# Summing the projection of an attention layer in half-height TensorE tiles, with denser keys

## The reference

```python
qk = jnp.einsum('bhwc,oc->bhwo', x, W_qk) + b_qk      # q: 4 heads x 64, k: 32 channels
...
attn = jnp.einsum('bxyhcp,bxyhdp->bxyhcd', q, k)      # sum over the 64 pixels p of a window
attn = attn * temperature[None, None, None, :, None, None]
```

## Time and profile before

| what | us |
|---|---|
| median of 3 runs | 1118.27 |
| lowest and highest | 1116.99, 1118.3 |
| the profiled execution's own time | 1117.37 |
| its span, first to last instruction | 1115.4 |
| TensorE matmul busy, VectorE busy | 888.9, 845.1 |

### The profile page before, as it was taken

One profiled execution on the slowest core, in us unless ns is written; L12 is line 12 of the kernel. 1 busy time (PEld: TensorE's weight loads), 2 busy tenths in 40 slices (PEclk: granted clock), 3 DMA queues, 4 the chain that ended last, 5 costly groups with the idle time before them and its releaser, 6 DMA issues. The chain is left out here.

```text
span 1115.4 us, 21429 instructions
## 1 busy us (share of the span) xinstructions
PE 888.9 (80%) x6876; PEld 591.1 (53%) x6876; DVE 845.1 (76%) x1207; ACT 600.1 (54%) x695; POOL 324.9 (29%) x265
## 2 busy tenths in 40 slices
PE   5699986979997667965999949799966588676774
PEld 4343336978875465343433349788854563233332
DVE  7577787987868844885778879877778446799796
ACT  5899982323333153546999923233332444466564
POOL 0000008500009910510000067000089304465564
PEclk8899997989998678988999969999986688899897
DMA  9100000000000020242000000000000200033334
GB/s 304 36 1 0 0 0 1 0 1 1 0 1 2 1 75 3 72 139 88 0 0 0 0 1 1 1 1 0 1 2 2 75 0 1 0 114 113 113 113 151
DMA packets 51305, 39.40 MB, mean 35 GB/s; under 512 B 1600, under 2 KB 50880, under 8 KB 51008
## 3 DMA queue, kind: packets, MB, share of 16 engines
q1 hardware_dynamic: 51264, 38.85, 11.0%
HBM read 22.07 MB, written 16.78 MB: 35 GB/s over the span
## 5 line engine op out<-in xcount | busy, mean ns | idle before, releaser
L333 PE MATMUL ps<-work,cst 128*128 128x512 f32 x512 | 235.9, 608 | 17.3 <-ACT work L547 13.5
L333 PEld LDWEIGHTS ps<-work,cst 128*128 128x128 f32 x512 | 94.3, 193 | 157.6 <-issue 143.4
L547 ACT ACTIVATE work<-X,l0s 128x2048 f32 (+1 forms) x64 | 136.7, 2141 | 3.8 <-SPq L291 3.8
L253 PE MATMUL ps<-ST,work 128*128 128x512 f32 (+1 forms) x256 | 131.7, 638 | 7.5 <-DVE work L866 5.4
L554 ACT ACTIVATE work<-ps 128x2048 f32<-128x2048 f32 x64 | 123.1, 1924 | 7.1 <-PE ps L333 6.8
L988 POOL TENSOR_TENSOR work<-cst,ksum 128x512 f32<-128x512 f32 x64 | 69.5, 1105 | 174.5 <-SPq L291 172.6
L778 DVE TENSOR_TENSOR work<-ps,cst 64x512 f32<-64x512 f32 x128 | 88.1, 688 | 37.8 <-PE ps L400 36.0
L953 POOL TENSOR_TENSOR co<-mv,cst 128x1 f32<-128x1 f32 x8 | 1.5, 189 | 383.0 <-DVEq L243 296.7
L576 ACT ACTIVATE work<-ps 128x512 f32<-128x512 f32 x80 | 47.8, 597 | 99.6 <-PE ps L353 99.6
L1023 POOL TENSOR_TENSOR work<-X,work 128x512 f32<-128x512 f32 x64 | 82.1, 1286 | 58.9 <-DVE work L913 58.9
L364 PE MATMUL ps<-cst,work 128*128 128x143 f32 x640 | 96.5, 296 | 1.4 <-DVE X L728 1.2
(11 more groups left out here) (96 smaller groups left out, 1649.3 us busy)
## 6 DMA issues: line engine op xcount, KB each, us to landing
work<-x SPq DMA_DIRECT2D x32, 512.0 KB, 4.6
out<-work SPq DMA_DIRECT2D x64, 256.0 KB, 2.8
work<-choose SPq DMA_DIRECT2D x2, 2048.0 KB, 7.9
cst<-consts SPq DMA_DIRECT2D x1, 1009.5 KB, 9.0
cst<-consts SPq DMA_DIRECT2D x1, 64.0 KB, 1.9
```

Of the source, the lines that this page charges most:

```text
L253: return nc.tensor.matmul(ps[:, bank, :], sel[:, n, :], ST[:, ds(s * (4 * H), 4 * H)], start=True, stop=True)
L333: last = pe.matmul(ps[:, 4 * (m % 2) + b, :], wg[:, m, :], yb[:, m, b * BANK:(b + 1) * BANK], start=True, stop=True)
L547: act.activation(yb[:, m, :], X[:, ds(s * PIX + i * CHUNK, CHUNK)], ACT.Gelu, scale=l0s[:, m:m + 1], bias=l0s[:, MULTI + m:MULTI + m + 1]) ...
```

## The change

M is summed by one matmul for each pair, each half of the pixel rows and each image: 64 rows by 32 columns of the array, 33 columns moved. The upper half of the pixel rows gives the first window of a pair, the lower half the second, and each half has a PSUM bank of its own (4 + 2u + hp). The keys of a pixel are then just 32 numbers and a one, so `kh` has 33 columns where it had 128, `keys` is one operation over 128 partitions, and GpSimd sets only the ones. `copy_m` reads two banks in one operation. TensorE's middle banks are written out instead of looped.

```diff
@@ -138,7 +138,7 @@
         mall, _e0 = part(0, [NWIN, NWIN, C + 1])
         xn, _e = part(_e0, [RING, NWIN, WS, WS])
         xw, _e = part(_e, [RING, 4, P])
-        kh, _e = part(_e, [RING, 4, G, P])
+        kh, _e = part(_e, [RING, 4, G, C + 1])
 
         rs, _e = part(_e0, [RING, NWIN, P])
         qb, _ = part(_e, [RING, WS, NWIN // 2, WS])
@@ -190,7 +190,7 @@
         s_x1 = rsem("z_added", "dve")
         s_strip = sem("strip_ready")
         s_next = rsem("next_strip_ready", "pool")
-        s_zero = sem("keys_buffers_zeroed")
+        s_ones = sem("keys_ones_set")
         s_pt = sem("patches_transposed")
         s_pc = rsem("patches_copied", "act", DEEP)
         s_cv = rsem("pair_filtered", "pe", 2 * DEEP)
@@ -406,16 +406,18 @@
                     pe.wait_ge(s_kh, after(nn))
                     pe.wait_ge(s_mc, slot(nn))
                     for pp in range(4):
-                        for g in range(G):
-                            last = pe.matmul(ps[C * g:C * g + C, 4 + u, pp * P:pp * P + P],
-                                             xw[:, u, pp, C * g:C * g + C], kh[:, u, pp, g, :],
-                                             start=True, stop=True)
+                        for hp in range(2):
+                            rows = slice(N * hp, N * hp + N)
+                            for g in range(G):
+                                last = pe.matmul(ps[C * g:C * g + C, 4 + 2 * u + hp, pp * (C + 1):(pp + 1) * (C + 1)],
+                                                 xw[rows, u, pp, C * g:C * g + C], kh[rows, u, pp, g, :],
+                                                 start=True, stop=True)
                     last.then_inc(s_m, 1)
 
                 project(0, 0, 0, 0)
                 project(0, 1, 0, 1)
                 m_sum(0, 0)
-                with pe.Fori(0, 7) as i:
+                for i in range(7):
                     for u in range(2):
                         w1 = i * 2 + (u + 1)
                         project(w1, w1 * 2, 1 - u, 0)
@@ -588,8 +590,8 @@
                 def copy_m(n, u):
                     nn = s * NB + n
                     act.wait_ge(s_m, after(nn))
-                    src = ps[:, 4 + u, :].rearrange("p (a b) -> p a b", b=N)[:, :, 0:C + 1]
-                    dst = work[:, ds(n * (8 * (C + 1)), 8 * (C + 1))].rearrange("p (a b) -> p a b", b=C + 1)
+                    src = ps[:, 4 + 2 * u:6 + 2 * u, 0:4 * (C + 1)].rearrange("p hp (a b) -> p a hp b", b=C + 1)
+                    dst = work[:, ds(n * (8 * (C + 1)), 8 * (C + 1))].rearrange("p (a hp b) -> p a hp b", hp=2, b=C + 1)
                     act.activation(dst, src, ACT.Copy).then_inc(s_mc, 1)
 
                 copy_xw(0, 0)
@@ -770,15 +772,11 @@
                     nn = s * NB + n
                     dve.wait_ge(s_wt, nn + 1)
                     dve.wait_ge(s_m, slot(nn))
-                    for hp in range(2):
-                        rows = slice(N * hp, N * hp + N)
-                        k_in = ps[rows, 2 + u, :].rearrange("p (a g d) -> p a g d", a=4, g=G)
-                        bias = c("bk", rows).rearrange("p (o g d) -> p o g d", o=1, g=G).broadcast_to([N, 4, G, C])
-                        o = kh[rows, u, :, :, N * hp:N * hp + C]
-                        last = dve.tensor_tensor(o, k_in, bias, ALU.add)
-                    last.then_inc(s_kh, 1)
-
-                dve.wait_ge(s_zero, s + 1)
+                    k_in = ps[:, 2 + u, :].rearrange("p (a g d) -> p a g d", a=4, g=G)
+                    bias = c("bk").rearrange("p (o g d) -> p o g d", o=1, g=G).broadcast_to([P, 4, G, C])
+                    dve.tensor_tensor(kh[:, u, :, :, 0:C], k_in, bias, ALU.add).then_inc(s_kh, 1)
+
+                dve.wait_ge(s_ones, s + 1)
                 norm_windows(0, 0)
                 norm_windows(1, 1)
                 with dve.Fori(0, 7) as i:
@@ -962,11 +960,7 @@
                 coefficients(1)
                 stage_end(pool, s, 1)
 
-                pool.memset(kh[:, :, :, :, :], 0.0)
-                pool.drain()
-                for hp in range(2):
-                    last = pool.memset(kh[N * hp:N * hp + N, :, :, :, N * hp + C:N * hp + C + 1], 1.0)
-                last.then_inc(s_zero, 1)
+                pool.memset(kh[:, :, :, :, C:C + 1], 1.0).then_inc(s_ones, 1)
                 pool.drain()
 
                 for t in range(2, STRIPS):
```

## The result

The changed kernel takes 1109.41 us in the median of four runs (1108.20 to 1111.15), the kernel before 1118.04 in its four (1116.99 to 1118.30). The ratio is 0.9926, with an interval of 0.9909 to 0.9943: 8.6 us faster, where 1101 us and 16.9 us of gain were forecast. The profiled execution took 1111.15 us, with a span of 1109.3, the longest of its four; that of before took 1117.37. So the two traces have 6.2 us between them to explain.

A forecast was written before the change was run, and what follows sets the result against it. The prediction took TensorE to bound stage 3. m_sum's 7.5 us and keys' 0.95 gave 8.45 a pass, 16.9 in both, the other terms zero: 1101 us, range 1088 to 1112.

The forecast's parts named there:

- term 4: TensorE's stage 3 loop written out: branch instructions go, more code is fetched, nothing won or lost; zero.
- term 5: Start of stage 2: memset goes, TensorE's transposes start earlier, VectorE ends later; zero, ends -3.0 to +4.8 us a pass.
- the rival with the strips in front: Stage 2: GpSimd's strips get in front of VectorE, 4.8 us a pass on top of the forecast, 1111 us; chance 0.2.
- Term 1: Stage 3: m_sum's loads take 0.55 us in place of 0.81, 0.25 us less a bank, 7.5 us a pass.
- A fixed price of 25 ns a record: Stage 3 rival: m_sum's 64 matmuls cost 25 ns each, 1.62 us together, about 1167 us in all; chance 0.01.
- Term 2: Stage 3: one keys operation fewer a bank, worth nothing mid-stage; last m_sum starts earlier, 0.95 us a pass.
- Term 3: Stage 3: copy_m reads as many numbers from two banks, 390 ns, with ScalarE far from full; zero.
- Stage 4 is written out already and its blocks keep their pace: Step given as evidence that fetching more code for stage 3's written-out loop costs zero.
- both parts of L751 first, as GpSimd's request comes just when the second follows the first: Start of stage 2: assumed order, then one strip, then L257, with VectorE done at 181.1; counted as zero.
- The rival of the clock: Stage 3: short streams in m_sum drop TensorE's granted clock to 1.2 GHz, around 1150 us; chance 0.02.

The follow-up runs named there:

- a_keys2: The changed kernel with wide keys (128 columns apart) in two operations and the old memsets, keeping only m_sum's small tiles; 1112.76 us, 0.9965.
- b_unroll: The kernel before with only TensorE's middle banks of stage 3 written out instead of looped; 1116.15 us, 0.9991.
- a_cols128: The changed kernel with keys 128 columns apart, all 128 moved in m_sum, and a memset of 4096 columns; 1118.35 us, a single execution.
- a_two: The changed kernel with one more small GpSimd memset, setting the column of ones to zero first; 1092.85 us, 0.9791.
- a_zero: The changed kernel with a GpSimd memset of 4096 columns put back in front of the strips; 1101.37 us, 0.9874.
- a_poolwait: The changed kernel with GpSimd's first strip in stage 2 waiting for VectorE's three normalisations; 1096.36 us, 0.9815.
- pw_loop4b: a_poolwait with TensorE's middle banks in a loop of four and m_sum's waits before the last matmul of the project ahead; 1098.98 us, 0.9833.
- pw_warm2: a_poolwait with three idle TensorE matmuls, two at the end of stage 3 and one after stage 4's first r_sum; 1095.16 us, 0.9807.
- a_cols66: The changed kernel with keys 66 columns apart, all 66 moved in m_sum, and a memset of 2112 columns; 1099.60 us, a single execution.
- pw_two: a_poolwait with the extra small memset of a_two; 1090.22 us, 0.9754.
- all_three: pw_two with the three idle TensorE matmuls of pw_warm2; 1084.40 us, 0.9696.

## Where the prediction held, and where it failed

The direction held, and the time lies in the range (1088 to 1112), but the forecast of 16.9 us was twice the 8.6 measured. The two terms that carry the gain, m_sum and keys, are right as mechanisms. What failed are two terms that were put at zero: term 4, the loop written out, and term 5, the start of stage 2. A third cost, the clock in stage 4, the sum did not have. The time also lies near the 1111 us of the rival with the strips in front, and its mechanism came true. That the number fits so well is luck: the rival has 9.6 us for stage 2, of which the stages show 4.1, and the rest of the way are pauses and the clock. By its own steps, against the profiled execution:

- **Term 1, m_sum: right in mechanism, under-sized.** The block went from 1.01 to 0.69 us, 0.32 less instead of 0.25. The loads took 0.65 where 0.55 was put down, since records start 10 ns apart and not at the 6.9 of the fastest burst. Against that, the 0.20 us before the next project were taken as fixed and are gone. The gap is there at 128 columns and not at 33, so it belongs to the width of the last matmuls. 30 banks at 0.32 are 9.6 us a pass instead of 7.5. A fixed price of 25 ns a record would have made 1.6 us of the 64; the trace has 0.65, and from 17 to 66 columns only 0.07 us more. The Trainium skill, page "TensorEngine Tiling (Array Packing)", section "Instruction Overhead", gives each matmul an overhead of some 60 cycles, at 2.4 GHz an estimate of the same 25 ns; for m_sum's records in eight tiles the trace does not agree.
- **Term 2, keys: right** at the end of the stage: the last m_sum follows the one ahead without a gap in pass 1, while in a_keys2 it waits 0.84 us. In the middle, a bank of a_keys2 without a pause takes 2.17 us with the wide keys too, as forecast.
- **Term 3, copy_m: right**, 391 ns and no wait on it in the groups.
- **Term 4, the loop written out at zero: failed.** It costs 3.3 and 1.8 us in pauses. "Stage 4 is written out already and its blocks keep their pace" is no evidence for stage 3, whose banks had become short: with the long banks of b_unroll and a_cols128 the same step would have been right. That the pauses are waits for code is the reading of three things: no semaphore is waited for within an m_sum, each pause ends 1.2 to 1.7 us after a fetch, and short code in a loop has no fetch and no pause but at its edge. The loop is not a way out, as its edges cost 3.6 to 3.8 us a pass. The Trainium skill, page "Runtime: NRT & Kernel Launch", section "Instruction fetch mechanics", has code fetched in blocks of 16 KiB and calls the cost of a new block mostly hidden. The trace agrees in the size (58 fetches, 0.95 MB) and, for b_unroll, in the cost; for the short banks it does not.
- **Term 5, stage 2 at zero: failed**, within its bounds of -3.0 to +4.8: it cost 2.0 and 2.1 us a pass. The step that failed is "both parts of L751 first, as GpSimd's request comes just when the second follows the first". The request, at 174.52, came while the short part (174.26 plus 0.5) was still running, and a strip went in at each of the two boundaries. VectorE was through 3.5 us later than before; the stage lost only 2.0, since before TensorE's clock came up late enough to cost 1.4; against b_unroll the changed kernel loses 3.4 and 3.3 us a pass. In a_two the request came at 174.92, during the long part. That is the order of the forecast, VectorE ends 0.1 us later than before, and the stage takes what it takes in b_unroll: for that order zero was right.
- **Not foreseen: stage 4**, 1.9 and 1.8 us, by the granted clock. The rival of the clock was priced for stage 3 alone, where it did not fall (0.95 and 0.96, with the pauses in it); what it did in the stage behind was not asked.

The sum for stage 3: 9.6 + 0.95 is 10.6 us a pass, less pauses of 3.3 and 1.8 gives 7.3 and 8.8, where the stage lost 7.0 and 8.4. The sum over the stages: -15.4 for stage 3, +4.1 for stage 2, +3.8 for stage 4, +2.4 for the start and stage 1, -1.0 for the stages behind, -6.1 in all, as between the two spans. The medians differ by 8.6; the profiled execution was the slowest of its four, and the start and stage 1 are where the traces vary by themselves.

## What to carry to other kernels

When a matmul block is cut shorter, price the number of records, the handover to the next block, and what the longer block was hiding: here, code that must be fetched or a loop's edge. Where two engines exclude each other, removing work of one does not free the other; the next operation of the first moves forward, and the order of the requests decides, so write the order down with a wait. Read the granted clock of the stage behind the one that was changed, and compare the clock before the times of two stages are compared: here it moved stage 2 by 1.4 us with nothing in it edited.

## What was not expected of the hardware

**The waiting engine goes in at the next boundary.** VectorE's three operations stand back to back, yet a strip of GpSimd that has been waiting goes between each two, some 3.4 us later each time (L753 5.38 instead of 2.00, L257 5.42 instead of 2.03). The Trainium skill, page "SBUF — State Buffer", section "SBUF: two separate sides", has the exclusive port; the traces agree, and they add who gets it next.

**The output stage has two patterns.** Its two lines in the changed kernel:

```profile
L911 DVE SCALAR_TENSOR_TENSOR work<-work 128x512 f32<-128x512 f32 x64 | 92.2, 1446 | 0.0
...
L1017 POOL TENSOR_TENSOR work<-X,work 128x512 f32<-128x512 f32 x64 | 82.3, 1288 | 58.7 <-DVE work L911 58.7
```

and in a_two:

```profile
L911 DVE SCALAR_TENSOR_TENSOR work<-work 128x512 f32<-128x512 f32 x64 | 83.4, 1308 | 0.0
...
L1019 POOL TENSOR_TENSOR work<-X,work 128x512 f32<-128x512 f32 x64 | 92.8, 1467 | 38.9 <-DVE work L911 38.9
```

Nothing in that stage was edited. In the first GpSimd is the quicker and waits 58.7 us for VectorE; in the second VectorE is the quicker, GpSimd takes longer for each and waits less, and the stage with the output ends after 183.5 us instead of 192.7. A chunk of it takes 1.67 us (in a_zero) where it takes 2.07 before and after. The traces show the long form, 191.5 to 193.6 us, before and after the change and in a_poolwait, pw_loop4b and pw_warm2 among others. They show the short one, 183.4 to 184.3 us, in a_zero, a_two, a_cols66, a_cols128, pw_two and all_three, all of which have two memsets of GpSimd at the start of stage 2. With one (the changed kernel) and with three (before, a_keys2) it is the long form. With the wait in place the second memset still separates them, a_poolwait from pw_two. The runs of a_zero spread from 1098.69 to 1111.53 us, as if both forms occurred in them. Whether the cause is where GpSimd's code lies or a small shift in time stays open; 9 us hang on it, as much as on the whole change.
